# Batch 1's rows, query and key tiles and values moved into the first steps of attention

## The reference

```
x = x + 0.5 * ffn(layernorm(x))        # top-1 routing to 8 experts, capacity 512 rows each
x = x + attention(layernorm(x))
x = x + 0.5 * ffn(layernorm(x))

attention:  q, k, v = x @ wq.T, x @ wk.T, x @ wv.T           # 16 heads of 16
            q, k = rope(g * q * rsqrt(mean(q*q) + eps)), the same for k
            y = softmax(q @ k.T / 4 + 1) @ v;   y @ wproj.T
```

## Time and profile before

| | us |
|---|---|
| median of 3 runs | 2191.47 (2187.69 to 2192.53) |
| the profiled execution | 2189.99 |
| its span, first to last instruction | 2188.2 |
| first maximum of step 0 | at 331.43 |
| first maximum of step 20, with the first exponentials | at 389.70 |
| first maximum of step 38 | at 447.85 |
| last maximum ends | at 1892.0 |

### The profile page before, as it was taken

How to read it: one execution, slowest core, us unless ns; L and a number is a source line. 1 busy time by engine, 2 the same in 40 slices (tenths; PEclk the granted TensorE clock), 3 DMA queues, 4 the chain that set the end, 5 groups by cost and what they waited for, 6 DMA issues and landing times.

```text
span 2188.2 us, 39171 instructions
## 1 busy us (share of the span) xinstructions
PE 2102.1 (96%) x14431; PEld 1077.7 (49%) x14431; DVE 1733.0 (79%) x2562; ACT 1679.8 (77%) x3251; POOL 990.6 (45%) x1221
## 2 busy tenths in 40 slices
PE   5799999999999999999999999999999999997997
PEld 4589874434444344344443444443444333246997
DVE  7777768888879888988988898889789998536674
ACT  5566646798888888888888888888888888755664
POOL 5787427652741672285158226713840101104542
PEclk9799998999999999999999999999999999999999
DMA  7454415245344344334443434443353335103331
GB/s 254 151 192 141 148 37 131 41 100 99 67 98 84 80 96 106 64 75 122 76 90 72 105 64 93 89 88 69 73 125 51 68 60 118 41 23 123 120 121 63
DMA packets 137855, 208.91 MB, mean 95 GB/s; under 512 B 30527, under 2 KB 95295, under 8 KB 137408
## 3 DMA queue, kind: packets, MB, share of 16 engines
q1 hardware_dynamic: 129792, 189.14, 36.5%
q0 software_dynamic: 7680, 16.87, 2.4%
q10 hardware_dynamic: 192, 0.39, 0.1%
HBM read 128.87 MB, written 72.01 MB: 92 GB/s over the span
## 4 chain that ended last, share of the span: by engine, by line
PE 74%; DVE 8%; ACT 2%; issue 1%; DMA 0%; POOL 0%; SPq 0%; another core or an unknown queue 0%; POOLq 0%; ACTq 0%; DVEq 0%
PE PS L1136 22%; PE PS L1119 18%; PE PS L1102 13%; PE PS L1009 6%; DVE NMX L2358 5%; PE PS L1073 3%; PE PS L816 3%; PE PS L971 1%; PE PS L973 1%; PE PS L972 1%; PE PS L951 1%; PE PS L953 1%; PE PS L952 1%; PE PS L1144 1%; ACT PB L1539 1%
## 5 line engine op out<-in xcount | busy, mean ns | idle before, releaser
L2358 DVE TENSOR_REDUCE NMX<-PS 128x1 f32<-128x1024 f32 x1024 | 1225.6, 1218 | 223.4 <-PE PS L1102 213.5
L1539 ACT ACTIVATE PB<-PS 128x512 f32<-128x512 f32 x2048 | 1104.3, 603 | 161.7 <-PE PS L1119 123.3
L1119 PE MATMUL PS<-QF,KF 51*128 51x512 f32 x2048 | 777.6, 457 | 6.2 <-ACT PB L1539 3.4
L1102 PE MATMUL PS<-KF,QF 49*128 49x512 f32 x2048 | 732.8, 445 | 10.1 <-DVE NMX L2358 9.5
L1136 PE MATMUL PS<-PB,V 128*17 128x512 f32 (+1 forms) x5512 | 577.0, 490 | 0.2
L1119 PEld LDWEIGHTS PS<-QF,KF 51*128 51x128 f32 x2048 | 317.2, 184 | 443.1 <-ACT PB L1539 235.7
L1102 PEld LDWEIGHTS PS<-KF,QF 49*128 49x128 f32 x2048 | 309.8, 185 | 165.7 <-DVE NMX L2358 95.8
L1136 PEld LDWEIGHTS PS<-PB,V 128*17 128x17 f32 x5512 | 91.6, 95 | 223.0 <-issue 155.6
L2001 DVE TENSOR_TENSOR HLR<-HL,HHR 128x512 fp32r<-128x512 f32 x128 | 92.5, 724 | 86.0 <-ACT HHR L1465 79.0
L2734 POOL TENSOR_TENSOR R1R<-R,HI 128x512 fp32r<-128x512 f32 x62 | 79.4, 1282 | 148.4 <-ACT R L1502 148.3
L971 PE MATMUL PS<-W2H,HLR 128*128 128x256 f32 x512 | 143.2, 280 | 0.0
(11 more groups left out here) (346 smaller groups left out, 3108.6 us busy)
## 6 DMA issues: line engine op xcount, KB each, us to landing
W<-in_w SPq DMA_DIRECT2D x32, 1024.0 KB
QF<-qs SPq DMA_DIRECT2D x186, 128.0 KB
KF<-qs SPq DMA_DIRECT2D x186, 128.0 KB
qs<-HI SPq DMA_DIRECT2D x64, 256.0 KB, 2.1
qs<-R1R SPq DMA_DIRECT2D x62, 256.0 KB, 2.3
QX<-x2d SPq DMA_DIRECT2D x8, 1024.0 KB, 5.3
out_x<-QX SPq DMA_DIRECT2D x8, 1024.0 KB, 4.9
YT<-YU SPq DMA_DIRECT2D x124, 64.0 KB, 4.0
```

The costliest lines, as they stand in the source:

```text
L1102: m = e.matmul(PS[:, 2 * i + half, :], QF[k][at:at + ROWS_S, p * SEQ + ti * 128:p * SEQ + ti * 128 + 128], KF[k][at:at + ROWS_S, p * SEQ + ...
L1119: e.matmul(PS[:, bank, :], KF[k][at:at + ROWS_ST, p * SEQ + sbk * 128:p * SEQ + sbk * 128 + 128], QF[k][at:at + ROWS_ST, p * SEQ + th * 51 ...
L1539: e.activation(PB[j % 3][:, h * 512:(h + 1) * 512], PS[:, place["e", tile], :], ACT.Exp).then_inc(e_out, 1)
L2358: e.tensor_reduce(NMX[:, u % 2, at:at + 1], PS[:, 2 * i:2 * i + 2, :], AX.XY, ALU.max, negate=True).then_inc(s_max, 1)
```

## The change

Nothing that is computed changes. The timetables do, and some places of storage:

- Batch 1 gets a timetable of its own, `NEXT`, in steps of the loop: statistics at steps 0 to 2, normalizing at step 4, transposes at 6 and 7, its eight query and key tiles at steps 8 to 15, seven of its value tiles at 16 to 20 and the last at 25. Squares, sums, rotation, roots, splits and stores of batch 1 stay in order behind it, at `QK_AT` and `PIECES` counted from step 6.
- The eight tiles lie in `QK1`, eight buffers in place of the ring of three, over `YU`, `YT` and `SB`. These are first written at steps 29 to 44, and their writers now wait on `rope_free`. ACT copies a tile at its step and squares it from `QK1` later. `PX1` (batch 1's rows) moves to where the ring lies, and its load is issued in `lead()`.
- POOL's `lead()` takes batch 1's inverse after the third rotated tile of batch 0, roots and scales batch 0's tiles 0 to 3 at once, and forms the low parts of batch 1's rows between tiles 4 to 7.
- Batch 0's last four splits move from steps 13, 14, 15, 17 to 11, 13, 18, 21, their stores from three steps behind to one. `load_unit(2)` moves from step 21 to 24. The ones of units 1 and 2 are written in eight pieces at steps 7 to 19, and three sums of batch 0 later.
- The dummy matmuls stay in steps 0 to 7 only.
- For all batches `XT_AT`, `QK_AT`, one entry of `VALUES_AT`, `HALVED` (23 entries before, 27 after) and a few due times of the routing (`LATER`, `SOONER`) are set anew by a step or less, in `QK_AT` by up to two.

```diff
-XT_AT = (9, 10, 11, 12)
-QK_AT = (16, 18, 19, 22, 24, 27, 28, 30)
+XT_AT = (8, 10, 12, 13)
+QK_AT = (16, 17, 19, 22, 25, 27, 30, 32)
-VALUES_AT = (52, 54, 56, 58, 60, 64, 66, 68)
+VALUES_AT = (52, 54, 56, 58, 60, 65, 66, 68)
-PIECES_0 = ((0, 0, 2), (0, 0, 0), (1, 1, 2), (1, 1, 0), (13, 1, 1), (14, 1, 3), (15, 0, 1), (17, 0, 3))
+PIECES_0 = ((0, 0, 2), (0, 0, 0), (1, 1, 2), (1, 1, 0), (11, 0, 1), (13, 0, 3), (18, 1, 1), (21, 1, 3))
+NEXT = dict(stats=(0, 0, 0, 1, 1, 1, 2, 2), mean=(2, 2.5), sums=(2, 6, 7, 7, 8), normal=(4, 4, 4, 4, 4, 4, 4, 4),
+            across=(6, 6, 7, 7), both=(8, 9, 10, 11, 12, 13, 14, 15), values=(16, 16, 17, 17, 18, 19, 20, 25),
+            ones=(7, 8, 9, 10, 14, 14, 17, 19))
-HALVED = (1, 2, 3, 9, 11, 15, 20, 23, 24, 26, 27, 28, 41, 43, 47, 49, 51, 55, 56, 57, 58, 59, 60)
+HALVED = (0, 2, 3, 9, 17, 20, 23, 24, 26, 27, 28, 33, 36, 41, 43, 47, 49, 50, 51, 52, 55, 56, 57, 58, 59, 60, 63)
-AGAIN_AT = {n: 4 for n in range(LAG + 1)}
+AGAIN_AT = {n: 4 for n in range(8)}
...
-        PX1 = put("PX1", [128, 8, 256], here=pb_at + 4096)
+        PX1 = put("PX1", [128, 8, 256], here=0)
+        QK1 = put("QK1", [128, 8, 512], here=pb_at + 6144)
...
@@ SP
+                load_px(1)                                    # lead(), behind batch 0's rows
-                    yield 5
+                    yield 8 if u == 1 else 5                  # load_unit(u + 1)
+                if u < 3:                                     # gather(u), before YT is written
+                    e.wait_ge(rope_free, (4, 4, 6)[u])
+                if u == 0:                                    # spread(0), before SB is written
+                    e.wait_ge(rope_free, 8)
@@ PE
-                busy[bank] = (qk_sq, n + 1)
+                busy[bank] = (qk_out, n + 1) if b == 1 else (qk_sq, n + 1)
@@ ACT, batch 1
+                    e.copy(QK1[:, t, :], PS[:, place["qk", n], :]).then_inc(qk_out, 1)
...
+                    e.wait_ge(qk_out, n + 1)
+                    e.wait_ge(sq_sum, n + 8)
+                    e.activation(SQ[:, :], QK1[:, t, :], ACT.Square).then_inc(qk_sq, 1)
...
+                for i in range(8):                            # the ones
+                    yield NEXT["ones"][i]
+                    if i == 4:
+                        e.wait_ge(rq_root, 4)
@@ POOL, lead()
+                    if t == 3:
+                        inverse(0, pn_ve, pn_rs, 4)
+                        own.out(e.tensor_tensor(DV[:, 1, :], VE[:, 0, :], RS[:, 0, :], ALU.mult))
+                        rooted(0)
+                    if t >= 4:
+                        across_low(1, t - 4)
+                rooted(1)
```

More of the change, by code:

```diff
@@ L1472, in pre_x @@
             def pre_x(b):
-                if b == 1:
-                    yield from normalized([lambda i: PX1[:, i, :]] * 2, lambda i: RS[:, 0, i:i + 1], 0, pn_rs, b + 4, pn_xn,
-                                          [8 + i // 2 for i in range(4)])
                 for g in range(4):
-                    yield XT_AT[g]
+                    yield NEXT["across"][g] - BEGIN[1] if b == 1 else XT_AT[g]
                     e.wait_ge(xt_full, 4 * b + g + 1)
@@ L1481, in pre_x @@
                     e.copy(XTP[:, :, g * 256:(g + 1) * 256], src).then_inc(xt_raw, 1)
-                for t in range(8):
+                for t in range(8 if b == 1 else 0):
+                    yield NEXT["both"][t] - BEGIN[1]
+                    n = 8 + t
+                    e.wait_ge(qk_full, n + 1)
+                    if t == 0:
+                        e.wait_ge(sq_sum, 16)
+                    e.copy(QK1[:, t, :], PS[:, place["qk", n], :]).then_inc(qk_out, 1)
+                for t in range(8 if b == 1 else 0):
+                    yield QK_AT[t]
+                    n = 8 + t
+                    e.wait_ge(qk_out, n + 1)
+                    e.wait_ge(sq_sum, n + 8)
+                    e.activation(SQ[:, :], QK1[:, t, :], ACT.Square).then_inc(qk_sq, 1)
+                for t in range(8 if b > 1 else 0):
                     yield QK_AT[t]
@@ L1550, in weighed @@
                         e.wait_ge(ld_rc, 64 * u)
+                    else:
+                        e.wait_ge(rope_free, th + 1)
                     e.copy(YU[:, th, :], PS[:, V_BANK, :]).then_inc(pv_out, 1)
@@ L1700, in second_pair, with next_rows @@
                 load_pair(e, KF[0], D, PIECE_K, 1, ld_u[0])
-                for k in range(1, 3):
-                    ones(k)
+                for i in range(8):
+                    yield NEXT["ones"][i]
+                    if i == 4:
+                        e.wait_ge(rq_root, 4)
+                    k, t, half = 1 + i // 4, i // 2 % 2, i % 2
+                    part = slice(32 + 64 * half, 64 + 64 * half)
+                    m = e.copy((QF, KF)[t][k][part, :], ONES[part, 0:1].to_broadcast([32, 2 * SEQ]))
+                    if half:
+                        m.then_inc(set_act, 1)
+            def next_rows():
+                for i in range(8):
+                    yield NEXT["normal"][i]
+                    if i == 0:
+                        e.wait_ge(pn_rs, 6)
+                    e.activation(PX1[:, i, :], PX1[:, i, :], ACT.Identity, scale=RS[:, 0, i:i + 1],
+                                 bias=NB_[:, 0, i:i + 1]).then_inc(pn_xn, 1)
             lead()
@@ L1709, in scalar_program @@
                     side.begin(n, second_pair())
+                    side.begin(n, next_rows())
                     prepare(side, BEGIN[1], 1, pre_x, split, values)
@@ L2034, in here @@
                     if i == 0:
-                        e.wait_ge(ld_px, 16 * (b + 1))
+                        e.wait_ge(ld_px, 16 * b)
                         e.wait_ge(pn_rs, b + 4)
-                yield from moments(0, lambda i: px_of(b)[:, i, :], [i // 2 + (2 if b == 1 else 0) for i in range(8)], (6, 6) if b == 1 else (4, 4), here, pn_ve)
+                if b == 1:
+                    at = [k - BEGIN[1] for k in NEXT["stats"]], [k - BEGIN[1] for k in NEXT["mean"]]
+                else:
+                    at = [i // 2 for i in range(8)], (4, 4)
+                yield from moments(0, lambda i: px_of(b)[:, i, :], *at, here, pn_ve)
                 for t in range(8):
@@ L2175, in summed_later @@
                 for t in range(3, 8):
-                    yield t - 3
+                    yield NEXT["sums"][t - 3]
                     summed(t, 1)
@@ L2685, in normalized, with across_low @@
                                     ).then_inc(xn, 1)
+            def across_low(b, g):
+                part = slice(g * 256, (g + 1) * 256)
+                e.wait_ge(xt_raw, 4 * b + g + 1)
+                e.tensor_tensor(XTL[:, :, part], XTP[:, :, part], XTH[:, :, part].bitcast(F32), ALU.subtract
+                                ).then_inc(xt_lo, 1)
             def lead():
@@ L2724, in lead, with rooted @@
                             lower(k, k // 2)
-                for m in range(2):
-                    root(m, 1)
+                    if t == 3:
[5 more added lines that the diff above has]
+                rooted(1)
+            def rooted(m):
+                root(m, 1)
                 own.wait(e)
-                e.wait_ge(rq_root, 4)
-                for t in range(8):
+                e.wait_ge(rq_root, 3 + m)
+                for t in range(4 * m, 4 * m + 4):
                     scale_half(e, t, 1)
@@ L2736, in pre_x @@
             def pre_x(b):
-                yield 6 if b == 1 else 4
-                inverse(0, pn_ve, pn_rs, b + 3)
-                own.out(e.tensor_tensor(DV[:, b % 3, :], VE[:, 0, :], RS[:, 0, :], ALU.mult))
                 if b > 1:
+                    yield 4
+                    inverse(0, pn_ve, pn_rs, b + 3)
+                    own.out(e.tensor_tensor(DV[:, b % 3, :], VE[:, 0, :], RS[:, 0, :], ALU.mult))
                     px = lambda i: PX[:, i, :]
@@ L2743, in pre_x @@
                     normalized(px, px, 0, pn_xn)
-                for g in range(4):
+                for g in range(4 if b > 1 else 0):
                     yield XT_AT[g] + 1
[L2746 to L2749, removed]
+                    across_low(b, g)
                 for t in range(8):
```

39 lines of the change are left out of this document (19 added, 20 removed).

## The result

The changed kernel takes 2164.63 us, median of 4 executions (2162.91 to 2166.20). The kernel before took 2192.0 in 4 (2187.69 to 2197.87). The ratio is 0.986, 95% interval 0.983 to 0.989, so it is faster by 27 us.

What follows compares the result with a forecast made beforehand. DVE was taken to bound steps 0 to 19, PE the later ones. Terms -8.5, -0.6, -4.7 and +0.2 sum to -13.6 us, giving 2176.4 from the profile, 2177.9 from the median; forecast 2178, range 2168 to 2187.

Steps and rivals of the forecast that it cites:

- The other batches: Later batches: shifted tiles up to +3.5 us, halved steps +6.4 to -16, all taken as 0.
- Rival 4: Six later batches: halved steps and spread tiles gain 1 us a batch, total 2171 us; chance 15%.
- The slow clock goes and the collisions take its place: Steps 0 to 19: slow-clock waits end, PE's side work makes DVE wait instead; 58.5 us against 58.27, cost 0.2.
- a wait for unit 1's heads: Step 16: PE waits about 1 us for unit 1's load, landing at 376.5 but wanted at 375.4.
- rival 1: Steps 8 to 19: with dummies removed the clock stays low, slower than before, 2197 us, 5%; a short fall 8%.
- short form: Steps 4 to 7 or so: the clock falls only briefly, costing 3 to 5 us, total 2182; chance 8%.
- long form: Steps 8 to 19: all twelve run at 1.2 GHz, stretch 19 us longer, total 2197; chance 5%.
- The tiles: Steps 20 to 37 and 58 to 65: bare steps of 2.58 us remain, value tiles 0.75 each; gains 8.5 and 4.7.
- Rival 3: DVE's early steps: PE's room is as small as its busy share, tiles cost 1.4 each, +8, 2186 us; 5%.
- The chain that must keep up: Queues of ACT, POOL and SP: tiles, low parts and loads come in time, except about 1 us for unit 1.
- rival 2: ACT or POOL comes late and PE waits; three or four lapses make 6 us, total 2184; chance 17%.

Runs made afterwards that it cites:

- The tables alone: The kernel before with the new XT_AT, QK_AT, VALUES_AT, HALVED, LATER and SOONER, batch 1's work not moved; 2181.17 us, ratio 0.9939.
- the move alone: The changed kernel with XT_AT, QK_AT, VALUES_AT, HALVED, LATER and SOONER as before; 2181.35 us, ratio 0.9925 to the kernel before.

## Why the prediction was wrong

Term by term, by the profiled executions:

| term of the sum | predicted | measured |
|---|---|---|
| steps 0 to 19 | +0.2 | +3.1 |
| steps 20 to 37 | -8.5 | -9.8 |
| steps 38, 39 | -0.6 | +0.3 |
| steps 40 to 57 | 0 | +0.2 |
| steps 58 to 65 | -4.7 | -5.6 |
| steps 66 to 511 | 0 | -14.5 |
| before step 0, and behind the last maximum | 0 | +2.6 |

**The step that failed** is "The other batches", where I wrote "I take 0 for all of it". Steps 66 to 511 gave 14.5 us: 1.7 in the rest of batch 1, 2.95 in each of batches 2 to 5 and 2.4 in batch 6, less 1.4 in batch 7, in which the clock fell. (Batch 1 as a whole gave 3.9, but 2.2 of that are its steps 64 and 65, which belong to the value tiles' term.) The tables alone, without the move, gave 15.6 in steps 66 to 511, so the gain is theirs. My ground was that the bounds stood on both sides (+6.4 to -16 for the halved steps alone). Zero is not what bounds on both sides say; the middle of +6.4 and -16 is -5. The working was wrong, too: I priced a halved step by PE's busy time, 0.2 dearer, where the distance from maximum to maximum is 0.38 shorter in step 50. And I said that no row sets a halved and a whole step side by side. But the waits of DVE for the second score tile (0.36 in step 50 before) were in the trace, and each of them was a candidate. The sign of being wrong that the prediction had set for this, later batches that move by over 1 us each, came. Rival 4, given 15%, had the mechanism right ("the halved steps and the spread tiles gain"), with a third of its size.

**Steps 0 to 19.** "The slow clock goes and the collisions take its place" was half right. DVE waited 9.4 us in steps 0 to 19 (61.33 - 51.92), where I had 7.0. In steps 7 to 19 the collisions cost 4.6; I had 6.0 for steps 6 to 18 and, beside it, 1.0 for a wait for unit 1's heads. That wait is the only one of its kind in the list of waits of steps 0 to 19, half of what I said:

```profile
PEld PS L1112 <- DMA KF<-qs: 0.5, 1, 0.5
```

The slow clock did not go. The side condition named in rival 1, that steps 2 to 5 hold the least PE work, decided: the fall came at the end of step 2 or in step 3, and cost 4.7 us of DVE's time in steps 3 to 6. It is that rival's short form, "steps 4 to 7 or so, costs 3 to 5", given 8%; filling takes 3.1 to 3.8 off the stretch. Its long form did not come: the clock was 1.00 from step 7 to the end of batch 6. The Trainium skill, TensorE: Matmul & The Clock Gate, The HAM clock gate, says that throttled is the default and that activity releases it. By that rule dummies belong where the engine is thin. The runs agree: twelve in step 2 left the clock at 1.00 in steps 0 to 19, and four more in each of steps 8 to 19 left it at 0.90.

**The tiles.** That a query and key tile leaves 2.58 us behind when it goes was right and a little too dear: 18 steps took 48.3 for 49.7. The value tiles gave 5.6 for 4.7; with the move alone 5.1, so 0.5 of it is the tables'. Rival 3, that PE's room is as small as its busy share, is excluded: eight tiles of 1.58 us and the rest of the side work went into steps 7 to 19 for 4.6 us, with PE busy at 35.17 of 36.16. Steps 38 and 39 did not give their 0.6, with ACT busy for 6.31 of 6.35 us; with the move alone they took 5.89 and gave 0.2, so the tables cost 0.5 there.

**The chain that must keep up** held. ACT and POOL do not appear in the list of waits of PE for steps 0 to 19 with over 0.3 us in any entry, so rival 2 did not come.

**The sum against the move alone.** The sum had worked out the move and nothing else, 13.6 us. By the medians the move alone gave 14.0, by the loop's time 11.1: 3.1 worse than the sum in steps 0 to 19, 1.1 better in the later stretches, 0.6 worse in steps 66 to 511. So the sum was right to some 2.5 us for what it held, partly by luck, since its errors have both signs, and the rest of the miss is the tables. What no term held is that move and tables help each other, by 4.6 us in the profiles: batch 0 is where the tables cost something, and the move takes nearly all of that cost away.

**What stays open.** Which pair of tables makes the last 0.4 us of a batch was not run. Whether it is the length of the gap in step 2 or the little work of the whole step that goes with the fall was not told apart. The changed kernel's first set (2164.63) is 5.9 above its second (2158.77). In the first set's profile the clock also stood at 0.50 for 7 us at 1705, in the second's not, and batch 7 took 179.11 against 175.52, which is 3.6 of it; why it fell there was not tried.

## What to carry to other kernels

A timetable entry that looks trivial is multiplied by the batches: price one batch step by step, from the distance between two pacing instructions and the waits between them, and never put zero for a term only because its bounds have both signs. Put dummies where the pacing engine holds TensorE longest, not evenly. And look for the one place where an edit hurts (here the first batch), for another edit may remove just that place.

## What the runs showed of the hardware

- One gap of 1.72 us on TensorE, with 2.33 us of matmuls in a step of 4.00, went with a fall to 1.2 GHz of 14 us in all four profiles that have it, starting within 2 us of the gap's end. With the gap filled by eight more matmuls of 128x512 in bf16 (12 in 2.76 us, 0.23 each) no fall was seen in batch 0's steps in three profiles, two of which had two more in each of steps 3 to 5. 48 dummies more in steps 8 to 19 did not prevent it, as they come behind it, and cost 5.6 us.
- In step 50, weighing matmuls cut in two let the score tile behind it start sooner and took a DVE wait of 0.36 us away (step 2.71 to 2.34 us); 0.2 of that came back four steps later.
- With the clock at 1.00, identical rounds repeat to 0.12 us: batches 2 to 5 within 0.05 in the changed kernel. So one profile resolves parts of 0.2 us a batch that lie below what whole executions resolve.
